# Query scores of the next batch ahead of this batch's key scores, in each pair of heads, in a cross-attention kernel

## The chip, the cores and the metric

The kernel runs on one core of one Trainium2 chip. The metric is the device time of one launch in microseconds (us); lower is better. The profile's span is the time from the first to the last recorded instruction of one execution.

## What is computed

For each of B = 16 batch entries: 256 query rows x of width 320, and 256 context rows of width 512, of which the first 248 are text keys and the last 8 are four "dummy" and four "ip" keys. There are 20 heads of 16.

```python
q = _split_heads(hidden_states @ w_q, HEADS)
k = _split_heads(text @ w_k, HEADS)
v = _split_heads(text @ w_v, HEADS)
out_text = _merge_heads(_sdpa(q, k, v))
mask_ip = _ip_mask(bbox, B, S, hidden_states.dtype)
k_ip = _split_heads(ip_h @ w_k_ip, HEADS)
v_ip = _split_heads(ip_h @ w_v_ip, HEADS)
out_ip = _merge_heads(_sdpa(q, k_ip, v_ip, mask=mask_ip))
out = out_text + IP_SCALE * out_ip
out = out @ w_out + b_out
out = out + residual
```

`_sdpa` is softmax(q k^T / 4 + mask) v, and each of the two softmaxes subtracts the maximum of its own keys.

## The kernel before, in words

Every value goes through TensorE in f32r, and precision is kept by splitting numbers into a high and a low part. The projections of batch entries to q, k and v are made for two entries at a time, in ten **tiles** per group (three of k, four of v, three of q; names `tile`, `k_tile`, `v_tile`, `q_tile`, lines 689 to 699). A tile of k or q is evacuated in two steps: ScalarE copies the high part (line 474), and VectorE, which waits for that copy, subtracts it from the accumulator to get the low part (line 587; lines 581 and 584 for a narrow tile). A v tile needs ScalarE alone (lines 467, 469). The parts go out to DRAM and come back as stacks (`q_stack`, `k_stack`, `stack2`) in which a pair of heads lies on 128 partitions, 64 for each.

Attention works on ten **pairs** of heads, p = 0 to 9, per batch entry t. Scores are made twice:

- **query scores** of entry t + 1 (`query_scores`, matmuls of line 743, queries on the partitions of the accumulator `score_q`): VectorE takes from them the maximum over each query's keys (`maxima`, lines 595 and 597). The maxima are turned and carried through DRAM into rows of the q stack, so that
- **key scores** of entry t (`key_scores`, matmuls of line 804, keys on the partitions, accumulator `score_t`) come out with the maximum and the mask already in them. ScalarE makes exp of them (line 520) into `probs`.

Each group of either kind is four matmuls of 256 columns with 64 rows of weights. `values` (line 819, 24 matmuls, once for two pairs, at even p) multiplies `probs` with v. ScalarE copies the result out (line 512), VectorE turns it and inverts the sums (lines 642, 645), GpSimd normalises (lines 434, 439), VectorE turns it back (line 650), TensorE projects (`project_out`, line 828), and VectorE adds the residual (line 657).

The order of all of it is written by hand in `batch(t)`, once for each engine, and every engine works its own list in order. On TensorE a pair p of step t is: key scores of (t, p); query scores of (t + 1, p); at even p the values; at p = 3, 5 and 9 the output projection of entry t - 1; at odd p, while t is up to 11 ("hosted"), a whole projection tile. On ScalarE a pair is: exp of the key scores, then (even p) the high part of a tile, then the copy of the values' result, then at some p the split of raw inputs (lines 454, 458). On VectorE it is: the maxima, at p = 4 and 9 a small turn (line 603), the low part of a tile, line 650, lines 642 and 645, line 657, and the split of inputs (lines 564, 568, 570) at p = 6 and 9 of odd t and p = 8 of even t.

The waits that tie them: a query group waits for `max_done`, the maxima of the pair before (for the pair before that one where there are two banks of `score_q`, entries 13 to 15, that is steps 12 to 14). A key group waits for `exp_done`, the exp of the pair before, since `score_t` is one buffer; at p = 0 and 5 also for the rows of maxima (`rows_loaded`). Values wait for the exp of pair p - 1. Query pair 1 of entry 13 also waits for the last two hosted tiles to be evacuated.

Of the kernel before, what the change touches and what calls it, by code (L numbers as in the profile page):

```python
# [34 lines left out]
def xattn(nc, x, xT, ctxT, ctx_sp, bbox, wq, wk, wv, wk_ip, wv_ip, wo, bias, grid, kaux, vones, out):  # L35
# [12 lines left out]
    with ctx:  # L48
# [67 lines left out]
        def double(b):  # L116
            return b == 0 or b - 1 > LAST_HOST
# [4 lines left out]
        def score_bank(b, p, e):  # L122
            return score_both(b, p)[:, 512 * e:512 * e + 512]
# [53 lines left out]
        def need(eng, s, value):  # L177
            if not isinstance(value, int) or value > 0:
                eng.wait_ge(s, value)
# [5 lines left out]
        def q_cols(w, p, e, a, n):  # L185
            return q_stacks[w][HEAD * e:HEAD * e + HEAD, p * S + a:p * S + a + n]
        def k_cols(w, p, e, a, n):
            return k_stacks[w][HEAD * e:HEAD * e + HEAD, p * KEYS + a:p * KEYS + a + n]
# [6 lines left out]
        def there(b):  # L195
            return 0 <= b < B
        def hosted(t):
            return -1 <= t <= LAST_HOST
# [5 lines left out]
        def tile_freed(eng, n):  # L204
            g, j = n // TILES, n % TILES
            if 3 <= j < 7:
                eng.wait_ge(v_evac, 4 * g + j - 2)
            else:
                eng.wait_ge(lo_done, 6 * g + (j if j < 3 else j - 4) + 1)
# [476 lines left out]
        def _(pe):  # L686
# [38 lines left out]
            def query_scores(b, p):  # L725
                n = PAIRS * b + p
                if p == 0:
                    pe.wait_ge(stack_loaded[b % 3], 112 * (b // 3 + 1))
                    if b == 0:
                        pe.wait_ge(kaux_loaded, 48)  # L730
                if p == 0 or not double(b):
                    need(pe, max_done, n)
                elif n - 1 > 0:
                    pe.wait_ge(max_done, n - 1)
                if p == 1 and b == 0:
                    for n_t in (12, 13):
                        tile_freed(pe, n_t)
                if p == 1 and b == LAST_HOST + 2:
                    for back in (1, 2):
                        tile_freed(pe, TILES * GROUPS - back)  # L740
                for tile in range(2):
                    for e in range(2):
                        last = mm(score_bank(b, p, e)[:, tile * KEYS:(tile + 1) * KEYS],  # L743
                                  q_cols(b % 3, p, e, tile * P, P), k_cols(b % 3, p, e, 0, KEYS), start=True, stop=True)
                last.then_inc(sq_ready, 1)
            def tile(n):
                g, j = n // TILES, n % TILES
                if g < 1 and j in (0, 3, 7):
                    pe.wait_ge(w_low, {0: 1, 3: 2, 7: 3}[j])
                if j == 7:  # L750
                    pe.wait_ge(x_tail, g + 1)
                if n < LONE:
                    if n >= 5:
                        tile_freed(pe, n - 5)
                else:
                    tile_freed(pe, n - (1 if n == LONE else 2))
                out = tile_bank(n)
                if j < 3:
                    k_tile(g, j, out)
                elif j < 7:  # L760
                    v_tile(g, j - 3, out)
                else:
                    q_tile(g, j - 7, out)
# [26 lines left out]
            def key_scores(b, p):  # L790
                if b == 0 and p == 0:
                    pe.wait_ge(max_done, PAIRS)
                if p % HALF == 0:
                    pe.wait_ge(rows_loaded[p // HALF], 16 * (b + 1))
                if b < B - 1 or p == 0:
                    need(pe, exp_done, PAIRS * b + p)
                elif p == 1:
                    pe.wait_ge(max_done, PAIRS * B)
                else:
                    pe.wait_ge(exp_done, PAIRS * b + p - 1)  # L800
                both = key_bank(b, p)
                for tile in range(2):
                    for e in range(2):
                        last = mm(both[:, 512 * e + S * tile:512 * e + S * tile + S],  # L804
                                  k_cols(b % 3, p, e, tile * P, P), q_cols(b % 3, p, e, 0, S), start=True, stop=True)
                last.then_inc(st_ready, 1)
            def values(b, k):
                u = b % 2
                if k == 0:
                    pe.wait_ge(v_spread, 2 * (b + 1))  # L810
                    pe.wait_ge(vsp_loaded[u], 8 * (b - u) + 16)
                need(pe, o_evac, QUADS * b + k)
                pe.wait_ge(exp_done, PAIRS * b + 2 * (k + 1))
                for kind in range(3):
                    tile = min(kind, 1)
                    for t in range(4):
                        a = (t % 2) * 2 * S + tile * S
                        at = S if kind == 2 else 0
                        last = mm(pv[32 * t:32 * t + 32, at:at + S], values_of(u, kind, 4 * k + t),  # L819
                                  probs[:, slot(u, 2 * k + t // 2), a:a + S],  # L820
                                  start=kind != 1, stop=kind != 0)
                last.then_inc(pv_ready, 1)
            def project_out(b, t, c):
                if t == 0:
                    pe.wait_ge(o_ready, OC * b + c + 1)
                if c == 0:
                    need(pe, out_done, OT * b + (t if b < B - 1 else 0))
                last = mm(out_bank(b, t), o_norm[:, b % 2, c, t * P:t * P + P], wo_sb[:, c, :],  # L828
                          start=c == 0, stop=c == OC - 1)
                if c == OC - 1:  # L830
                    last.then_inc(out_ready, 1)
            def batch(t):
                if t == 0:
                    pe.wait_ge(ld["small"], 32)
                    for back in range(1, 6):
                        tile_freed(pe, LONE - back)
                    pe.wait_ge(preset, 10)
                for p in range(PAIRS):
                    if there(t):
                        key_scores(t, p)  # L840
                    if there(t + 1):
                        query_scores(t + 1, p)
                    for k, off in VALUES.get(p, ()):
                        if there(t + off):
                            values(t + off, k)
                    for m, k in (OUT if t < B else LAST_OUT).get(p, ()):
                        if there(t - 1):
                            project_out(t - 1, m, k)
                    if hosted(t) and p % 2:
                        tile(5 * (t + 4) + p // 2)  # L850
            for t in range(-1, B + 1):
                batch(t)
# [57 lines left out]
```

## Time and profile before

| what | us |
|---|---|
| three runs | 506.11, 508.80, 510.87; median 508.8 |
| the profiled execution's own time | 508.77 |
| its span | 506.9 (1.9 us of the time lie outside it) |
| TensorE matmuls busy | 465.9 (92% of the span) |
| TensorE weight loads busy | 319.7 (63%) |
| VectorE busy | 391.2 (77%) |
| ScalarE busy | 275.3 (54%) |
| GpSimd busy | 154.1 (30%) |

PE is TensorE's matmuls, PEld its weight loads, DVE VectorE, ACT ScalarE, POOL GpSimd. Steps t = 0 to 15 begin with the key scores of their pair 0: step 1 at 108.66, step 3 at 166.16, step 4 at 193.09, step 12 at 419.45, step 13 at 440.35 and step 15 at 480.42.

### The profile page before, as it was taken

Reading aid. Unit: us, or ns where it says so; the run is one execution under the profiler, and the core shown is the slowest. Engines: PE = TensorE matmul, PEld = TensorE weight load, DVE = VectorE, ACT = ScalarE, POOL = GpSimd, SP = SyncE. Lnnn points to the kernel's source line nnn. Section 1 sums busy time; section 2 is a strip of 40 time slices with the busy share of each in tenths; the row PEclk is TensorE's granted clock in tenths of the full one; section 3 lists DMA queues with packets and bytes.
Section 4 is the critical chain, followed back from the end, with each engine's and each line's share of the span. In section 5 each row is a group of like instructions: output and inputs, shape, how many; then the busy total and the mean of one; then the engine's idle time right before and its main releaser. Section 6 shows DMA issues by size and latency. Waiting matters only on the chain.

```text
span 506.9 us, 11023 instructions
## 1 busy us (share of the span) xinstructions
PE 465.9 (92%) x4250; PEld 319.7 (63%) x4250; DVE 391.2 (77%) x705; ACT 275.3 (54%) x357; POOL 154.1 (30%) x242
## 2 busy tenths in 40 slices
PE   2899486999999999999999999999999998889987
PEld 2698364676666766676667766676667765555543
DVE  3824484796978789697978789697978788999933
ACT  3733022565646476456645566556645555666672
POOL 4490010313304152313204142323204141533442
PEclk9989695999999999999999999999999999999999
DMA  8989996929486585929495675939495655483021
GB/s 270 292 219 232 328 290 188 318 66 306 135 257 205 148 259 162 328 75 319 132 276 185 188 239 151 328 79 308 131 283 180 194 181 156 156 263 87 7 58 53
DMA packets 96453, 101.80 MB, mean 201 GB/s; under 512 B 16896, under 2 KB 83504, under 8 KB 96400
## 3 DMA queue, kind: packets, MB, share of 16 engines
q1 hardware_dynamic: 95408, 98.92, 63.1%
q0 software_dynamic: 992, 2.17, 2.0%
q8 instruction: 34, 0.56, 0.5%
q14 instruction: 19, 0.16, 0.1%
HBM read 67.87 MB, written 33.23 MB: 199 GB/s over the span
## 4 chain that ended last, share of the span: by engine, by line
PE 66%; DVE 14%; issue 7%; DMA 7%; ACT 3%; SPq 2%; POOL 1%; POOLq 0%; ACTq 0%
PE pv L819 15%; PE pj L828 10%; PE score_t L804 10%; PE score_q L743 6%; DVE max_cols L595 5%; PE score_q L694 4%; PE score_q L689 3%; PE score_q L695 3%; PE score_q L691 3%; PE score_q L696 3%; PE score_q L690 3%; PE score_q L698 2%; DVE qk_out L587 2%; PE score_q L699 2%; DMA v_rows<-v_out 1%
## 5 line engine op out<-in xcount | busy, mean ns | idle before, releaser
L520 ACT ACTIVATE probs<-score_t 128x1024 f32<-128x1024 f32 x155 | 158.3, 1021 | 139.5 <-PE score_t L804 139.2
L595 DVE TENSOR_REDUCE max_cols<-score_q 128x4 fp32r<-128x992 f32 x155 | 183.1, 1181 | 65.4 <-PE score_q L743 64.8
L819 PE MATMUL pv<-probs,v_cur 128*32 128x256 f32 x1920 | 120.2, 383 | 2.2 <-ACT probs L520 2.1
L434 POOL TENSOR_TENSOR o_turned<-o_turned,inv_cols 128x256 f32<-128x256 f32 x80 | 53.9, 674 | 158.0 <-DVE inv_cols L645 157.9
L819 PEld LDWEIGHTS pv<-probs,v_cur 128*32 128x32 f32 x1920 | 54.6, 109 | 40.6 <-issue 3.2
L426 POOL TENSOR_TENSOR x_all<-x_all,bias_sb 128x640 f32<-128x640 f32 x16 | 25.0, 1564 | 137.6 <-DMA x_all<-in_x 137.6
L828 PE MATMUL pj<-wo_sb,o_all 128*128 128x320 f32 x186 | 63.2, 460 | 4.0 <-DVE o_all L650 3.9
L512 ACT ACTIVATE o_all<-pv 128x512 f32<-128x512 f32 x80 | 47.8, 598 | 30.0 <-PE pv L819 29.3
L642 DVE STREAM_TRANSPOSE o_turned<-o_all 128x512 f32<-128x512 f32 x80 | 55.5, 693 | 10.9 <-ACT o_all L512 10.9
L804 PE MATMUL score_t<-q_stack,k_stack 64*128 64x256 f32 x420 | 52.9, 330 | 7.3 <-ACT probs L520 5.9
L804 PEld LDWEIGHTS score_t<-q_stack,k_stack 64*128 64x128 f32 x420 | 31.6, 186 | 44.3 <-issue 35.7
L743 PE MATMUL score_q<-k_stack,q_stack 64*128 64x256 f32 x420 | 44.4, 289 | 9.6 <-DMA q_stack<-aux_rows 7.5
L828 PEld LDWEIGHTS pj<-wo_sb,o_all 128*128 128x128 f32 x186 | 31.3, 189 | 19.5 <-DVE o_all L650 7.1
L743 PEld LDWEIGHTS score_q<-k_stack,q_stack 64*128 64x128 f32 x420 | 32.8, 188 | 12.7 <-issue 10.3
L689 PE MATMUL score_q<-wv_hl,c_hi 128*128 128x320 f32 x112 | 39.6, 353 | 0.0
L439 POOL TENSOR_TENSOR o_all<-o_turned 128x128 f32<-128x128 f32 x80 | 37.6, 469 | 6.3
L691 PE MATMUL score_q<-wv_hl,c_hi 128*128 128x320 f32 x112 | 35.3, 315 | 0.0
L690 PE MATMUL score_q<-wv_hl,c_lo 128*128 128x320 f32 x112 | 35.2, 314 | 0.0
L597 DVE TENSOR_REDUCE max_cols<-score_q 128x4 fp32r<-128x32 f32 x155 | 27.9, 180 | 0.0
L804 PEld LDWEIGHTS score_t<-stack 64*128 64x128 f32 x200 | 14.9, 184 | 20.1 <-issue 16.6
L804 PE MATMUL score_t<-stack 64*128 64x256 f32 x200 | 25.2, 330 | 2.1 <-ACT probs L520 2.1
L474 ACT ACTIVATE qk_out<-score_q 128x512 fp32r<-128x512 f32 (+1 forms) x40 | 23.5, 588 | 3.8 <-PE score_q L695 3.3
(163 smaller groups left out, 683.3 us busy)
## 6 DMA issues: line engine op xcount, KB each, us to landing
k_stack<-k_parts SPq DMA_DIRECT2D x33, 320.0 KB, 5.0
q_stack<-q_parts SPq DMA_DIRECT2D x33, 320.0 KB, 5.5
q_parts<-qk_out SPq DMA_DIRECT2D x32, 256.0 KB, 4.7
k_parts<-qk_out SPq DMA_DIRECT2D x32, 248.0 KB, 5.2
raw<-in_ctxT SPq DMA_DIRECT2D x14, 512.0 KB, 4.5
v_rows<-v_out SPq DMA_DIRECT2D x32, 160.0 KB, 5.0
v_stage<-v_rows SPq DMA_DIRECT2D x16, 320.0 KB, 6.2
x_all<-in_x SPq DMA_DIRECT2D x16, 320.0 KB, 6.1
```

The costliest lines, as they stand in the source:

```text
L434: pool.tensor_tensor(out, out, inv_cols[:, n % SLOTS, :].unsqueeze(2).broadcast_to([P, 2 * S // 32, DH]), ALU.mult).then_inc(scaled, 1)
L512: nc.scalar.activation(o_raw[:, n % SLOTS, :], pv[:, :], ACT.Copy).then_inc(o_evac, 1)
L520: nc.scalar.activation(probs[:, slot(t % 2, p), :], key_bank(t, p), ACT.Exp, scale=SCALE)\
L595: nc.vector.tensor_reduce(out=max_cols[:, h, :, at:at + 4:2].rearrange("p t e -> p e t"), in_=both[:, :, :, 0:TEXT], op=ALU.max, axis=AX.X ...
L642: nc.vector.transpose(turned_blocks(n), o_raw[:, n % SLOTS, :].rearrange("p (j n) -> p j n", n=32))\
L689: mm(out, w_hi, x_hi_, start=start, stop=False)
L690: mm(out, w_lo, x_hi_, start=False, stop=False)
L691: return mm(out, w_hi, x_lo_, start=False, stop=stop)
L743: last = mm(score_bank(b, p, e)[:, tile * KEYS:(tile + 1) * KEYS], q_cols(b % 3, p, e, tile * P, P), k_cols(b % 3, p, e, 0, KEYS), start=T ...
L804: last = mm(both[:, 512 * e + S * tile:512 * e + S * tile + S], k_cols(b % 3, p, e, tile * P, P), q_cols(b % 3, p, e, 0, S), start=True, s ...
L819: last = mm(pv[32 * t:32 * t + 32, at:at + S], values_of(u, kind, 4 * k + t), probs[:, slot(u, 2 * k + t // 2), a:a + S], start=kind != 1, ...
L828: last = mm(out_bank(b, t), o_norm[:, b % 2, c, t * P:t * P + P], wo_sb[:, c, :], start=c == 0, stop=c == OC - 1)
```

## The change

In the pair loop of TensorE's `batch` the query scores of entry t + 1 stand ahead of the key scores of entry t. Nothing else is touched: the same instructions, waits and buffers, and the lists of the other engines are as before.

```diff
@@ -836,10 +836,10 @@
                         tile_freed(pe, LONE - back)
                     pe.wait_ge(preset, 10)
                 for p in range(PAIRS):
+                    if there(t + 1):
+                        query_scores(t + 1, p)
                     if there(t):
                         key_scores(t, p)
-                    if there(t + 1):
-                        query_scores(t + 1, p)
                     for k, off in VALUES.get(p, ()):
                         if there(t + off):
                             values(t + off, k)
```

## Rows read from the trace of the kernel before

**Rows 1.** The profile's page, part 1: TensorE's share of the span.
```profile
PE 465.9 (92%) x4250; PEld 319.7 (63%) x4250; DVE 391.2 (77%) x705; ACT 275.3 (54%) x357; POOL 154.1 (30%) x242
```
**Rows 2.** Windows of steps 3, 4 and 13: length, busy by engine, clock, DMA.
```profile
166.16:193.09 26.93, 26.85 (x259) 18.28 (x258) 22.34 (x43) 16.82 (x22) 8.72 (x14) 1.00 0.71 224
193.09:222.81 29.72, 29.23 (x271) 20.17 (x270) 25.11 (x45) 16.31 (x21) 8.41 (x13) 1.00 0.65 199
...
440.35:460.38 20.03, 17.94 (x213) 10.77 (x213) 18.75 (x39) 12.68 (x15) 7.61 (x13) 1.00 0.54 170
```
**Rows 3.** Waits from 109 to 419 us: total, times, longest.
```profile
PE pj L828 <- DVE o_all L650: 2.4, 5, 0.5
PEld score_q L743 <- DVE max_cols L597: 1.7, 6, 0.3
```
**Rows 4.** Timeline of TensorE, pairs 6 to 9 of step 3: start, length.
```profile
182.06 0.51 PE L804 MATMUL score_t<-q_stack,k_stack 64*128 64x256 f32 x4
182.41 0.40 PE L743 MATMUL score_q<-k_stack,q_stack 64*128 64x256 f32 x4
182.73 1.50 PE L819 MATMUL pv<-probs,v_cur 128*32 128x256 f32 x24
...
186.88 0.51 PE L804 MATMUL score_t<-q_stack,k_stack 64*128 64x256 f32 x4
187.24 0.51 PE L743 MATMUL score_q<-k_stack,q_stack 64*128 64x256 f32 x4
187.67 1.50 PE L819 MATMUL pv<-probs,v_cur 128*32 128x256 f32 x24
...
189.69 0.50 PE L743 MATMUL score_q<-k_stack,q_stack 64*128 64x256 f32 x4
190.12 0.81 PE L828 MATMUL pj<-wo_sb,o_all 128*128 128x320 f32 x2
```
**Rows 5.** Timeline of ScalarE, pair 6 of step 3.
```profile
182.61 1.03 ACT L520 ACTIVATE probs<-score_t 128x1024 f32<-128x1024 f32 x1 [1.22 <-PE score_t L804]
183.53 0.59 ACT L474 ACTIVATE qk_out<-score_q 128x512 fp32r<-128x512 f32 x1
```
**Rows 6.** Timeline of VectorE, pairs 6 to 8 of step 3.
```profile
182.85 1.19 DVE L595 TENSOR_REDUCE max_cols<-score_q 128x4 fp32r<-128x992 f32 x1 [1.00 <-PE score_q L743]
183.96 0.18 DVE L597 TENSOR_REDUCE max_cols<-score_q 128x4 fp32r<-128x32 f32 x1
184.16 0.69 DVE L587 TENSOR_TENSOR qk_out<-score_q,qk_out 128x512 fp32r<-128x512 f32 x1
184.77 1.22 DVE L564 TENSOR_TENSOR c_lo<-raw,c_hi 128x1024 fp32r<-128x1024 f32 x1
...
187.00 0.18 DVE L597 TENSOR_REDUCE max_cols<-score_q 128x4 fp32r<-128x32 f32 x1
...
189.45 0.18 DVE L597 TENSOR_REDUCE max_cols<-score_q 128x4 fp32r<-128x32 f32 x1
```
**Rows 7.** Timeline of TensorE, pair 9 of step 4.
```profile
218.80 0.50 PE L743 MATMUL score_q<-stack 64*128 64x256 f32 x4
```
**Rows 8.** Timeline of TensorE: query groups that waited, entries 1 and 2.
```profile
82.51 0.80 PE L743 MATMUL score_q<-k_stack,q_stack 64*128 64x256 f32 x4 [0.75 <-DVE max_cols L597]
...
109.66 0.50 PE L743 MATMUL score_q<-stack 64*128 64x256 f32 x4 [0.49 <-DVE max_cols L597]
```
**Rows 9.** Timeline of TensorE, step 12: query pair 1, projection at pair 3.
```profile
423.13 0.50 PE L743 MATMUL score_q<-k_stack,q_stack 64*128 64x256 f32 x4 [1.08 <-issue]
...
427.41 0.81 PE L828 MATMUL pj<-wo_sb,o_all 128*128 128x320 f32 x2 [0.47 <-DVE o_all L650]
```
**Rows 10.** Timeline of step 13: key groups of pairs 1 and 2, and exp between.
```profile
442.45 0.50 PE L804 MATMUL score_t<-q_stack,k_stack 64*128 64x256 f32 x4
...
443.08 1.02 ACT L520 ACTIVATE probs<-score_t 128x1024 f32<-128x1024 f32 x1
...
444.15 0.50 PE L804 MATMUL score_t<-q_stack,k_stack 64*128 64x256 f32 x4 [0.96 <-ACT probs L520]
```

## Prediction, made before the changed kernel was run

> **What bounds the kernel now.** First the busy shares of the page: TensorE's matmuls fill 92% of the span, VectorE 77%, ScalarE 54% [rows 1]. Since that is an average over stages, the second view is the windows by step. In steps 3 and 4, which have projection tiles in them, TensorE is busy 26.85 of 26.93 us and 29.23 of 29.72, VectorE 83% and 84%; in step 13, which has none, 17.94 and 18.75 of 20.03 [rows 2]. So steps 1 to 11 belong to TensorE: anything that makes it stand still is paid in full there. The last full steps are a chain among three engines. The third view is the waits of 109 to 419 us: query groups wait for maxima six times, 1.7 us in all, and the projection five times for line 650, 2.4 us [rows 3]. VectorE's wait for query scores is not on the path. The fourth view, the timelines, shows how close these waits are, and carries the sum.
>
> **What the swap moves.** No instruction is added. A key group starts at 182.06, the query group at 182.41, the values at 182.73: whichever group is first takes 0.34, the second 0.33, 0.67 together [rows 4]. Both have four matmuls of 256 columns with 64 rows of weights, so I take the same steps with the names exchanged. Then query scores end 0.23 earlier in a pair and key scores 0.23 later: the first group ends 0.51 after the pair's start, the second 0.75 (182.41 + 0.40 - 182.06 = 0.75; 0.75 - 0.51 = 0.24, and 0.23 between the starts of what reads them) [rows 4]. In TensorE's sum that is nothing. The question is who reads late or early.
>
> **Part 1, the wait that moves ahead of the key scores (steps 1 to 10).** Look at pairs 6 to 8 of step 3. ScalarE makes exp of pair 6 from 182.61, and only behind it the high part of the tile, 183.53 to 184.12 [rows 5]. VectorE ends its maxima of pair 6 at 184.14, starts the low part at 184.16, then the input split at 184.77, and so ends the maxima of pair 7 at 187.18; the query group of pair 8 starts at 187.24, 0.06 later [rows 4, 6]. Two things had to be ready for the low part at 184.16, the maxima (184.14) and the high part (184.12). The swap makes the first 0.23 earlier, as VectorE waited 1.00 us for the query scores [rows 6], and the second 0.23 later, because exp starts later. The later one decides: low part, split and maxima of pair 7 are all 0.23 late, and the maxima end at 187.41. Before, the key group (186.88) ran while TensorE waited for these maxima, and the values followed the query group by 0.43 (187.24 to 187.67) [rows 4]. Now the key group stands behind the wait: query 187.47, key 187.81, values 187.47 + 0.67 = 188.14. That is 0.47 late: 0.23 from the late exp, 0.24 from the lost cover.
>
> At pair 9 VectorE comes without a gap from the same chain, the maxima of pair 8 ending at 189.45 + 0.18 = 189.63. The query group moves from 189.69 to 189.92, and what follows from 190.12 to 190.59, again 0.47 in absolute time, so it is not paid twice [rows 4, 6]. From there to the next such place TensorE has its tile to do, VectorE catches up, and at pair 6 of the next step it again waits for the query scores. So the loss comes once in a step. In an even step the narrow tile stands in the place of tile and split, and it is at pair 9 that the query group waits (0.50 long, as a stalled one is, against 0.40) [rows 7]: 0.47 there too. In step 11 there is no input split, so I count nothing. Ten steps x 0.47 = **4.7 us**. The bounds: nothing, if the low part isn't late (then the 0.23 gained by the maxima just pays for the lost cover); 10 x 0.67 = 6.7, if a whole pair of groups is lost. I take 4.7, since both inputs of the low part are within 0.04 us of its start in the row.
>
> The projection of pair 5 waits for line 650, behind a low part [rows 3]. Between nothing and 5 x 0.23 = 1.2 us; the maxima ahead of it come 0.23 sooner, which nearly makes room for the later high part, so I take **0.3**.
>
> **Part 2, steps 0 and 1.** Query pair 1 of entry 1 waits for its maxima and starts at 82.51 [rows 8]; the key group of that step ran ahead of it, in idle time, and now follows. That costs between 0.34 and, the group there being 0.80 long where a stalled one elsewhere has 0.50 [rows 4, 8], about twice that; part comes back later, so **0.35**. At 109.66 pair 0 of entry 2 waits in the same way for maxima behind a split [rows 8]: 0.23 + 0.24 = **0.47**. Together 0.8 (bounds 0.3 and 1.2).
>
> **Part 3, steps 12 to 14.** In step 13 the key group of pair 2 (444.15) waits 0.96 for the exp of pair 1, which starts at 443.08, 0.13 after the end of the key group of 442.45 (442.95), where exp elsewhere follows by 0.04 (182.57 to 182.61): ScalarE is held by its copy of the values' result [rows 4, 5, 10]. After the swap that key group ends at 443.18 and exp starts at 443.23, 0.15 late. The next query group is then made inside the wait, so the values follow a lone key group by 0.43 instead of 0.67. Gain 0.67 - 0.43 - 0.15 = 0.09, at three of the five pairs of pairs: 0.27 in each of two steps, **-0.5**. If VectorE alone bounded these steps, 20.03 could fall towards its 18.75 [rows 2]: at most 1.3 each.
> Step 12 loses. Query pair 1 of entry 13 waits for the last tile's evacuation until 423.13 [rows 9], and the key group and its exp used to lie in that wait. Now they follow it: key, exp (1.02) and a lone key group before the values add up to about 1.5. The projection of pair 3 stood 0.47 for line 650 [rows 9] and more waits for exp follow, and VectorE is nearly full there, so most is absorbed: between 0 and 1.5, I take **+0.5**. The tail comes out at 0 (bounds -2.6 and +1.5). Step 15 has no query scores.
>
> **Sum.** 4.7 + 0.3 + 0.8 + 0 = +5.8 us on the profiled execution's 508.77 (its span and 1.9 us around it): **514.6 us**, +1.1%. That execution lies on the median of the runs shown, 508.8.
>
> **A page's rule against the rows.** VectorE at 83% is in step 3 well below TensorE's matmuls, but above its weight loads, 18.28 of 26.93 us or 68% [rows 2]. The Trainium skill, "Perfetto Trace Analysis", section "Identifying the Most-Contended Engine", says that busy matmuls are a bad measure of TensorE's headroom and that weight-load occupancy should be used. By it VectorE would be the contended engine and TensorE would have room for the late starts, and the sum would be near zero; by the rows, groups that follow one another without a gap, there is none. That is rival B.
>
> **The rivals.**
> A. The low part isn't late, since TensorE's ends in the trace are modelled and 0.04 us decides. Then maxima of pair 7 end at 186.95, query pair 8 starts at 187.01, and values at 187.68, as before; the same at pair 9. Parts 2 and 3 remain: about 509.6. For it: nothing but the smallness of the margin. Against: ScalarE works in order, and exp starts 0.04 after the key scores' end.
> B. The hosted steps have slack and nothing moves: 508.8. For it the share of weight loads; against it 26.85 of 26.93 us.
> C. Faster. In the last steps and wherever VectorE waits for query scores it gains 0.23 a pair. The mechanism is one: the maxima are VectorE's longest work, and if their chain set the pace of steps 12 to 14, these would fall from 20.0 towards 18.75 us, 3 x 1.3 = 3.9 us less, 505. It decides only if exp (ScalarE) isn't what holds pair 2 and if the hosted steps lose nothing; the row shows the wait for exp.
> D. The new standstills of steps 0, 1 and 12 bring TensorE's clock down from 2.4 to 1.2 GHz for a stretch. In the rows shown for the full steps the granted clock is 1.00, with hardly an idle microsecond [rows 2]; step 12 would have one idle stretch of about 1.6 us ahead of its second query group (1.08 in the row, and the 0.50 of the key group that leaves it) [rows 4, 9]. The price if some 4 to 7 us of matmuls run at half speed: 3 us more, 517.6.
>
> **How the numbers follow.** Forecast 0.68, A 0.14, B 0.05, C 0.05, D 0.08. A measurement of this kernel tells about 1%, 5.1 us, from no change, so the border is 513.9, close under the forecast. Of the forecast I put seven tenths above it (the hosted loss could as well be 4 as 5.5): 0.49, with D 0.57. Faster by over 1% needs all of C and more: 0.02. The rest, 0.41, is within 1%. The range: below it B and C, above it half of D; 509.3 to 517.2.
>
> **What would show it.** In the changed profile: (1) query group first in each pair, 0.34 to the key group; (2) at pair 6 of odd steps the tile's high part 0.23 later after the pair's start (1.47 to 1.70), the low part right behind it, with a small idle gap ahead of it on VectorE; (3) at pairs 8 and 9 idle time of TensorE ahead of the query group for maxima, and a total of such waits from 109 to 419 us of some 5 us more than 1.7; (4) step 3 at 27.4 and step 4 at 30.2 us; (5) step 13 at about 19.8; (6) values of step 12's first pairs 1.5 us late, mostly made good by its end. It would be wrong if steps 3 and 4 keep 26.9 and 29.7 (A or B), if low parts still start with the maxima's end (A), if steps 13 and 14 lose more than a microsecond each (C), or if a stretch at half clock appears past 109 us (D).

## The result, and the profile after

| | kernel before | changed kernel |
|---|---|---|
| median of 4 runs each, us | 508.07 | 514.92 |
| lowest and highest | 506.11, 510.87 | 513.68, 516.63 |
| span of the profiled execution | 506.9 | 512.5 |

The ratio of the times is 1.0133, with a 95% interval of 1.0074 to 1.0192: slower by 1.3%. The forecast was 514.6 us.

The busy shares of the page have hardly moved: the same work, spread over 5.6 us more.

```profile
span 512.5 us, 11023 instructions
...
PE 465.7 (91%) x4250; PEld 319.8 (62%) x4250; DVE 391.5 (76%) x705; ACT 281.0 (55%) x357; POOL 153.1 (30%) x242
```

The windows of steps 3, 4, 12 and 13 of the changed kernel (length, then the busy time of PE, PEld, DVE, ACT, POOL, the granted clock, DMA share and GB/s):

```profile
167.18:194.82 27.64, 26.57 (x258) 18.14 (x257) 22.61 (x43) 17.11 (x22) 7.97 (x14) 1.00 0.68 218
194.82:225.23 30.41, 29.42 (x269) 20.04 (x269) 25.23 (x45) 16.66 (x21) 8.23 (x13) 1.00 0.65 195
424.96:446.47 21.51, 18.10 (x213) 10.85 (x212) 19.47 (x38) 13.66 (x16) 7.62 (x13) 1.00 0.56 172
446.47:466.28 19.81, 18.04 (x213) 10.82 (x213) 18.69 (x38) 13.22 (x15) 7.61 (x13) 1.00 0.53 172
```

Steps 3 and 4 were 26.93 and 29.72 us with TensorE busy nearly throughout; they are now 27.64 and 30.41, and TensorE stands still for about a microsecond in each (1.07 and 0.99, against 0.08 and 0.49 before [rows 2]). Step 13 is 0.22 shorter than its 20.03 [rows 2]; step 14 went from 20.04 to 19.79. Step 12 went from 20.90 to 21.51. Step 11 has kept its 26.44.

What TensorE now waits for, from 109 to 425 us (total, times, longest):

```profile
PEld score_q L743 <- DVE max_cols L597: 34.5, 68, 1.2
...
PE score_q L743 <- DVE max_cols L597: 7.2, 20, 0.8
DVE qk_out L587 <- ACT qk_out L474: 6.9, 17, 0.5
PEld pj L828 <- DVE o_all L650: 5.7, 10, 0.8
DVE tail_rest L581 <- ACT qk_out L474: 4.4, 10, 0.5
...
PE pj L828 <- DVE o_all L650: 2.9, 5, 0.6
```

The matmuls of query groups wait for maxima twenty times, in every one of steps 1 to 10 and mostly twice, for 7.2 us in all. The row to set beside it, from 109 to 419 us of the kernel before, is that of the matmuls too:

```profile
PE score_q L743 <- DVE max_cols L597: 0.5, 1, 0.5
```

VectorE waits for the high part of a tile, 11.3 us over 27 times, which did not stand among the waits of before at all. (The weight loads' own total of 34.5 counts idle time of weight loads while matmuls still run, and isn't lost time. The 1.7 us in six waits of [rows 3] is such a row of weight loads.)

The timelines of pairs 6 to 9 of step 3 show the chain. TensorE:

```profile
183.07 0.50 PE L743 MATMUL score_q<-k_stack,q_stack 64*128 64x256 f32 x4
183.41 0.40 PE L804 MATMUL score_t<-q_stack,k_stack 64*128 64x256 f32 x4
183.75 1.50 PE L819 MATMUL pv<-probs,v_cur 128*32 128x256 f32 x24
...
188.74 0.50 PE L743 MATMUL score_q<-k_stack,q_stack 64*128 64x256 f32 x4 [0.79 <-DVE max_cols L597]
189.08 0.40 PE L804 MATMUL score_t<-q_stack,k_stack 64*128 64x256 f32 x4
189.41 1.50 PE L819 MATMUL pv<-probs,v_cur 128*32 128x256 f32 x24
...
191.19 0.50 PE L743 MATMUL score_q<-k_stack,q_stack 64*128 64x256 f32 x4 [0.28 <-DVE max_cols L597]
```

ScalarE, then VectorE:

```profile
183.85 1.02 ACT L520 ACTIVATE probs<-score_t 128x1024 f32<-128x1024 f32 x1 [1.28 <-PE score_t L804]
184.77 0.59 ACT L474 ACTIVATE qk_out<-score_q 128x512 fp32r<-128x512 f32 x1
```

```profile
184.72 0.18 DVE L597 TENSOR_REDUCE max_cols<-score_q 128x4 fp32r<-128x32 f32 x1
185.40 0.69 DVE L587 TENSOR_TENSOR qk_out<-score_q,qk_out 128x512 fp32r<-128x512 f32 x1 [0.49 <-ACT qk_out L474]
186.00 1.48 DVE L564 TENSOR_TENSOR c_lo<-raw,c_hi 128x1024 fp32r<-128x1024 f32 x1
187.41 1.18 DVE L595 TENSOR_REDUCE max_cols<-score_q 128x4 fp32r<-128x992 f32 x1
188.51 0.18 DVE L597 TENSOR_REDUCE max_cols<-score_q 128x4 fp32r<-128x32 f32 x1
```

Pair 6 starts at 183.07. Exp starts 0.78 after it (0.55 before [rows 4, 5]), the high part 1.70 after it (1.47 before), and the low part 2.33 after it, where it was 2.10 [rows 4, 6]. VectorE is free at 184.90 and stands 0.49 until the high part is there; before, the two came 0.02 apart. The query group of pair 8 starts 0.05 after the end of the maxima, with nothing ahead of it but idle time, and the key group is behind it.

### The profile page after: what moved, and what is told of

It reads as the page before. It is cut to its first block, busy times and chain, and to the rows that moved or that the text cites. A ratio compares the mean times of both kernels' runs of the same rounds, so it can differ in the third digit from the quotient of the medians.

```text
span 512.5 us, 11023 instructions
## 1 busy us (share of the span) xinstructions
PE 465.7 (91%) x4250; PEld 319.8 (62%) x4250; DVE 391.5 (76%) x705; ACT 281.0 (55%) x357; POOL 153.1 (30%) x242
## 4 chain that ended last, share of the span: by engine, by line
PE 64%; DVE 15%; issue 8%; DMA 6%; ACT 4%; SPq 1%; POOL 1%; POOLq 0%; ACTq 0%; DVEq 0%
PE pv L819 13%; PE pj L828 10%; PE score_q L743 10%; DVE max_cols L595 6%; PE score_t L804 6%; PE score_q L694 4%; PE score_q L695 3%; PE score_q L689 3%; PE score_q L696 3%; PE score_q L691 3%; PE score_q L690 3%; ACT qk_out L474 2%; PE score_q L698 2%; PE score_q L699 2%; DMA max_rows<-row_buf 2%
## 5 line engine op out<-in xcount | busy, mean ns | idle before, releaser
L743 PE MATMUL score_q<-k_stack,q_stack 64*128 64x256 f32 x420 | 53.4, 333 | 17.1 <-DVE max_cols L597 10.1
L512 ACT ACTIVATE o_all<-pv 128x512 f32<-128x512 f32 x80 | 47.8, 598 | 12.8 <-PE pv L819 11.3
L804 PE MATMUL score_t<-q_stack,k_stack 64*128 64x256 f32 x420 | 43.1, 283 | 3.5 <-ACT probs L520 3.5
L743 PEld LDWEIGHTS score_q<-stack 64*128 64x128 f32 x200 | 14.9, 185 | 21.5 <-DVE max_cols L597 14.4
L743 PE MATMUL score_q<-stack 64*128 64x256 f32 x200 | 25.0, 328 | 3.3 <-DVE max_cols L597 3.1
```

The costliest lines, as they stand in the source:

```text
L512: nc.scalar.activation(o_raw[:, n % SLOTS, :], pv[:, :], ACT.Copy).then_inc(o_evac, 1)
```

## The experiments

Step lengths below are read from key and query group starts in each trace. In the even steps up to 10 and in steps 11 and 14 they repeat between traces of the same order to a few hundredths, where whole times spread over 4 us, so most verdicts rest on them. Odd steps need one more number beside them, given below the table. All kernels use this scheme in the pair loop, with another condition in each:

```diff
+                    first = <condition>
+                    if there(t + 1) and first: query_scores(t + 1, p)
                     if there(t): key_scores(t, p)
+                    if there(t + 1) and not first: query_scores(t + 1, p)
```

| kernel, condition for query scores first | step 3 | step 4 | step 12 | step 13 | step 14 |
|---|---|---|---|---|---|
| before: never | 26.93 | 29.72 | 20.90 | 20.03 | 20.04 |
| changed: always | 27.65 | 30.41 | 21.52 | 19.81 | 19.79 |
| e1: not at pairs 8, 9 | 27.52 | 30.19 | 23.32 | 20.04 | 20.03 |
| e2: always; high part ahead of exp | 27.05 | 29.50 | 21.14 | 20.05 | 19.79 |
| e3: never; high part ahead of exp | 26.80 | 29.71 | 20.90 | 20.03 | 20.04 |
| e4: steps 13, 14 | 27.06 | 29.72 | 20.91 | 19.81 | 19.79 |
| e5: pair 6 of steps 1 to 10 | 27.15 | 29.91 | 20.90 | 20.04 | 20.03 |
| e6: pairs 8, 9 of steps 1 to 10 | 27.14 | 29.98 | 20.90 | 20.03 | 20.04 |
| e7: see below | 26.77 | 29.54 | 20.91 | 19.81 | 19.79 |
| e8: not in step 12 | 27.38 | 30.38 | 20.90 | 19.81 | 19.79 |
| e9: step 0 and pair 0 of step 1 | 27.19 | 29.72 | 20.90 | 20.05 | 20.03 |
| e10: steps 1 to 10 | 27.40 | 30.40 | 21.74 | 20.04 | 20.03 |
| e11: step 12 | 26.91 | 29.71 | 23.08 | 20.04 | 20.03 |

Odd steps vary by more than even ones, also where nothing was changed. They go with the length of the input split behind pair 6 (line 564): with the order of before in it, step 3 is 26.91 to 26.93 where that split took 1.22, 27.06 where it took 1.36 (e4), and 27.19 where it took 1.48 (e9). So odd steps are compared here at equal splits. The split of step 3 took 1.22 in the kernel before, e5, e6, e8, e10 and e11, 1.21 in e3, and 1.48 in the changed kernel, 1.59 in e1, 1.46 in e2 and 1.43 in e7.

**Giving back one half: key scores first at pairs 8 and 9.**

```diff
+                    first = p not in (8, 9)
```

> The change with the key scores first again at pairs 8 and 9 alone. Theory: the 0.47 us that a hosted step loses are two halves. One is that exp of the key scores, and behind it on ScalarE the tile's high part at pair 6, start 0.23 late; the other is that at pairs 8 and 9 the key group no longer covers the wait for the maxima. This kernel gives back the second half only. So step 3 (27.65 in the changed kernel, 26.93 before) comes to 27.2 to 27.4, step 4 (30.41, 29.72 before) to about 30.15, and at pair 6 the high part is still 1.7 us after the pair's start. Rival (the lost cover is all of it, the late exp harmless): steps 3 and 4 are back at 26.9 and 29.7.

The windows of steps 3 and 4:

```profile
168.47:195.99 27.52, 26.98 (x260) 18.27 (x259) 22.72 (x43) 17.21 (x22) 8.62 (x14) 1.00 0.68 219
195.99:226.17 30.18, 29.52 (x269) 20.08 (x269) 25.16 (x45) 16.56 (x21) 8.42 (x13) 1.00 0.65 196
```

Steps 5 and 7 are at 27.15, against 27.38 in the changed kernel and 26.91 and 27.16 before (step 7 of before has a split of 1.47); even steps at 30.16 to 30.22. Step 3 lies above the range expected, with a split that took 1.59 where steps 5 and 7 have 1.22. So the cover gives back 0.2, and a loss stays: the rival, that the cover is all of it, falls. The single time was 516.59 us, above the changed kernel's, because of steps 0 and 12; step 12 is taken up under e11.

**The two halves each by itself.** First pair 6 alone, then pairs 8 and 9 alone.

```diff
+                    first = 1 <= t <= 10 and p == 6
```

> Query scores first at pair 6 of steps 1 to 10 alone, the kernel before elsewhere. Nothing stands behind a wait that did not before, so only the late exp is left, which is 0.23 us at pair 6. Theory: the tile's high part and the low part behind it are 0.23 late, so are the maxima that pairs 8 (odd steps) and 9 (even steps) wait for: step 3 comes to 27.16 (or 0.25 more if its input split is one of the long ones) and step 4 to 29.95, 0.23 above the kernel before in each. Rival (the lost cover is all that costs): 26.93 and 29.72.

VectorE at pairs 6 and 7 of step 3:

```profile
183.23 0.18 DVE L597 TENSOR_REDUCE max_cols<-score_q 128x4 fp32r<-128x32 f32 x1
183.91 0.69 DVE L587 TENSOR_TENSOR qk_out<-score_q,qk_out 128x512 fp32r<-128x512 f32 x1 [0.49 <-ACT qk_out L474]
184.51 1.22 DVE L564 TENSOR_TENSOR c_lo<-raw,c_hi 128x1024 fp32r<-128x1024 f32 x1
```

The same 0.49 of waiting as in the changed kernel, at a single exchanged pair in the step. Step 3 is +0.22, step 4 +0.19. The single time was 509.89.

```diff
+                    first = 1 <= t <= 10 and p in (8, 9)
```

> Query scores first at pairs 8 and 9 of steps 1 to 10 alone. Theory: the chain through pair 6 is on time, and the key group no longer covers the wait for maxima: 0.24 a step, step 3 at about 27.17, step 4 at about 29.96. With the kernel that swaps pair 6 alone it adds up to the 0.47 forecast for a step. Rival (the late exp is all of it): 26.93 and 29.72.

Step 3 is +0.21, step 4 +0.26; the single time was 511.89. In step 3, with the same split of 1.22 in all three, the halves add up to 0.43, close to what a step was forecast to lose (0.47). In step 4 they add up to 0.45, while the full swap costs 0.69. The other 0.2 is not made at pairs 6, 8 or 9; it is taken up in the part on the prediction.

**Taking the late exp out of the low part's way.** On ScalarE, in the changed kernel, the tile's evacuation goes ahead of exp:

```diff
                 for p in range(PAIRS):
+                    n = tile_due(t, p) if t >= 0 or p else LONE - 1
+                    if n is not None:
+                        tile(n)
                     if there(t):
...
-                    n = tile_due(t, p) if t >= 0 or p else LONE - 1
-                    if n is not None:
-                        tile(n)
```

> The change, and on ScalarE at even pairs the tile's high part ahead of exp. Theory: the high part is then done before the maxima end, the low part starts with the maxima's end, 0.23 us earlier than before the change, and this gain pays for the lost cover. Steps 3 and 4 come to about 26.9 and 29.6 (27.65 and 30.41 in the changed kernel), and the time falls by 4.5 to 6 us against it, to 509 to 510.5: not above the kernel before by more than 0.5%. Exp at even pairs starts 0.1 us later or less, which nobody waits for. Rival (the lost cover is the whole loss): step lengths and time stay as in the changed kernel, 514 to 515.

Ten runs gave a median of 506.6 us against 508.55 for the kernel before, ratio 0.9975 (0.9952 to 0.9998), a result better than expected, though the interval reaches nearly to 1. ScalarE and VectorE at pair 6 of step 3 (in e2, e3 and e7 exp is L523):

```profile
181.16 0.60 ACT L474 ACTIVATE qk_out<-score_q 128x512 fp32r<-128x512 f32 x1 [0.60 <-PE score_q L695]
181.83 1.02 ACT L523 ACTIVATE probs<-score_t 128x1024 f32<-128x1024 f32 x1
```

```profile
182.70 0.18 DVE L597 TENSOR_REDUCE max_cols<-score_q 128x4 fp32r<-128x32 f32 x1
182.80 0.68 DVE L587 TENSOR_TENSOR qk_out<-score_q,qk_out 128x512 fp32r<-128x512 f32 x1
183.40 1.46 DVE L564 TENSOR_TENSOR c_lo<-raw,c_hi 128x1024 fp32r<-128x1024 f32 x1
```

The low part follows the maxima at once: it starts 1.75 after the pair's start, against 2.33 in the changed kernel and 2.10 before. Even steps fall to 29.48 to 29.50, below the 29.7 of before; odd steps lie between 26.79 and 27.08, those with a split of 1.22 or 1.23 at 26.79 and 26.80. So the loss is gone once nothing else holds the low part. Step 12 is 21.14. Step 13 has kept 20.05: its first key group starts 0.48 after the query group instead of 0.34, since its rows of maxima had not yet landed.

**The control: the same exchange in the kernel before.**

> Control: the kernel before, with the same exchange on ScalarE. Theory: there the low part of pair 6 is held by the maxima's end just as much (184.14 against 184.12 for the high part), so nothing is gained: steps 3 and 4 at 26.9 and 29.7, time within 0.4% of the kernel before. Rival (the high part held VectorE in the kernel before too, and the exchange gains by itself): 2 to 5 us less than before, in steps 1 to 10.

Ratio 1.0000 (0.9978 to 1.0022), and even steps as before, 29.70 to 29.74: the exchange on ScalarE gains nothing that whole times can tell. It isn't quite without effect. In step 3 the low part starts 1.99 after the pair's start instead of 2.10, so in the kernel before the high part held it by 0.1, and odd steps with a split of 1.21 are 26.79 and 26.80 against 26.90 to 26.93, some 0.12 less. Five such steps make 0.6 us, inside the interval.

Beside e3 the result of e2 reads more closely. In odd steps both have 26.80: there the swap gains nothing, its earlier maxima just paying for the lost cover. In even steps the swap brings 29.71 down to 29.50, and 0.21 of this is there by the start of pair 6 (18.28 after the step's start, against 18.49). It is the wait of the projection of pair 5. From 109 to 417 us, e3 first and e2 second:

```profile
PE pj L828 <- DVE o_all L650: 2.5, 5, 0.5
PE pj L828 <- DVE o_all L650: 1.3, 5, 0.3
```

**The last steps alone.**

```diff
+                    first = t in (13, 14)
```

> Query scores first in steps 13 and 14 alone. Theory: steps 0 to 12 have the lengths of the kernel before (within 0.1 us), steps 13 and 14 fall from 20.03 to 19.8, since exp starts 0.15 us late but the query group is made while TensorE waits for it; the time is 0.4 to 0.5 us below before, which no pair of runs can tell, only the step lengths. Rival (the gain in the last steps needs what the earlier steps changed): steps 13 and 14 at 20.0.

Steps 13 and 14 are 19.81 and 19.79, all others as before (507.67 us in one run). The gain of 0.22 and 0.25 belongs to these steps and needs nothing from the others. TensorE in step 13 of the changed kernel shows how it comes about:

```profile
448.92 0.40 PE L804 MATMUL score_t<-q_stack,k_stack 64*128 64x256 f32 x4
449.15 0.40 PE L743 MATMUL score_q<-stack 64*128 64x256 f32 x4
450.44 0.50 PE L804 MATMUL score_t<-q_stack,k_stack 64*128 64x256 f32 x4 [0.88 <-ACT probs L520]
450.87 1.50 PE L819 MATMUL pv<-probs,v_cur 128*32 128x256 f32 x24
```

The query group of pair 2 (449.15) is made in what was a wait for exp, and the values follow the key group by 0.43. Before, that wait was idle [rows 10].

**Step 12.** First the change without it:

```diff
+                    first = t != 12
```

> The change without step 12. Theory: step 12 is 20.9 again (21.5 in the changed kernel), because the key group and its exp lie again in the wait of the second query group; steps 13 and 14 keep 19.8; steps 1 to 10 keep the changed kernel's lengths. About 0.6 us less than the changed kernel. Rival (step 12's loss comes from what the steps before left late, not from the order in it): 21.5 stays.

Step 12 is 20.90, as before the change, so its loss comes from the order in it. (The single time, 516.02, carries a step 0 of 34.4 us.) Then step 12 alone:

```diff
+                    first = t == 12
```

> Query scores first in step 12 alone. Theory: step 12 at 21.5 instead of 20.9, +0.6 us in time, which 5 rounds tell at best just. Rival (the idle stretch ahead of the second query group brings the clock down in some executions, as in the kernel with the key scores first at pairs 8 and 9, where step 12 took 23.3 with a half-clock stretch in it): a mean price above 1 us, and single executions that are 1.8 us longer.

Twelve runs: median 509.51 against 508.55, ratio 1.0018 (0.9996 to 1.0041). The execution that was profiled shows the rival's case. Windows of its step 12, the eighth column being the granted clock:

```profile
419.50:423.20 3.70, 1.17 (x18) 0.94 (x14) 3.22 (x6) 1.75 (x3) 0.00 (x0) 0.98 0.24 56
...
423.10:426.50 3.40, 3.40 (x28) 1.45 (x28) 2.30 (x5) 1.02 (x1) 1.08 (x2) 0.50 0.84 249
426.50:440.47 13.97, 13.09 (x144) 7.86 (x140) 12.76 (x26) 9.57 (x11) 5.50 (x9) 1.00 0.57 188
```

and its TensorE:

```profile
421.21 0.50 PE L743 MATMUL score_q<-k_stack,q_stack 64*128 64x256 f32 x4 [1.65 <-issue]
...
423.06 0.80 PE L804 MATMUL score_t<-q_stack,k_stack 64*128 64x256 f32 x4 [0.88 <-ACT probs L520]
423.79 2.79 PE L819 MATMUL pv<-probs,v_cur 128*32 128x256 f32 x24
```

TensorE stood idle for 1.65 us and again for 0.88, was busy 1.17 of 3.70 us, and then its clock was 0.50, that is 1.2 GHz, for 3.4 us: the values took 2.79 us instead of 1.50. Step 12 came to 23.08, of which 0.62 is the order (21.52 - 20.90) and some 1.6 the clock. e1 shows the same, 23.32 with a clock of 0.52 from 430.6 to 434.0. In the profiled execution of the changed kernel itself TensorE did the same before this point, and the clock stayed at 1.00:

```profile
427.07:430.77 3.70, 1.17 (x18) 0.93 (x16) 3.22 (x6) 1.75 (x3) 0.00 (x0) 1.00 0.24 57
```

In e2, with idle stretches of 1.27 and 0.88 there, it stayed up as well. So the fall comes in some executions and not in others. How often isn't shown: the twelve times of e11 lie between 508.41 and 513.52 and don't fall into two groups.

**Step 0 alone.**

```diff
+                    first = t == 0 or (t == 1 and p == 0)
```

> Query scores first in step 0 and at pair 0 of step 1 alone. Theory of the prediction: +0.8 us (509.2 against 508.4), since the key groups of these two places no longer run inside a wait. Rival: from the start of step 0 to pair 2 of step 1 the kernels with the old order there took 36.7 to 38.1 us, and three with the new order 37.8, 39.2 and 39.6, so the price is nearer to 1.6 us; or this is the spread of the loads and of the clock's half-speed stretch there, and the price is nothing that 5 rounds can tell (under 0.2%).

Median 508.86 against 508.55, ratio 1.0011 (0.9990 to 1.0031). That is +0.5 us with an interval from -0.5 to +1.6: it agrees with 0.8 and can't be told from nothing; a price of 1.6 is at its edge. From the start of step 0 to pair 2 of step 1 the kernels with the old order there took 36.7 to 38.1 us, those with the new order 36.9 to 39.6 (e9 itself 37.5), and e10, which has the new order in step 1 but not in step 0, 38.3. What makes that spread wasn't tried.

**Steps 1 to 10 alone.**

> Query scores first in steps 1 to 10 alone. Theory: the whole hosted loss and nothing else, steps 2 to 10 as in the changed kernel (27.4 and 30.4), +4.9 us in step lengths, time 513 to 513.8 against 508.4, ratio 1.009 to 1.011; steps 12 to 14 as before the change. Rival (steps 0 and 12 to 14 carry a good part of the 5 to 7 us measured): ratio under 1.008.

```diff
+                    first = 1 <= t <= 10
```

Ratio 1.0101 (1.0060 to 1.0142), median 513.80 against 508.55: +5.2 us, nearly all of what the change costs, and its step lengths are those of the changed kernel. Its step 12, untouched by the edit, was 21.74. The pairs of this step lie where they did in the kernel before, and the time is lost at its end, where the first key group of step 13 waits for its rows of maxima to come back from DRAM:

```profile
448.96 0.50 PE L804 MATMUL score_t<-q_stack,k_stack 64*128 64x256 f32 x4 [0.77 <-DMA q_stack<-max_rows]
```

The transfer that loads them was issued 19.64 us after the start of step 12, where the kernel before issued it after 18.21. Why it was late in this execution isn't shown.

**A version of it all.** High part ahead of exp; query scores first where it pays:

```diff
+                    first = t != 12 and not (t % 2 and t < 12 and p in (8, 9))
```

> High part ahead of exp on ScalarE; query scores first, but not in step 12 and not at pairs 8 and 9 of the odd steps up to 11. Theory: even steps keep the 29.48 that the kernel with the high part first has; odd steps gain the 0.23 as well, since maxima are earlier and the key group covers the wait again: about 26.7; step 12 is back at 20.9, steps 13 and 14 at 19.8. Together some 3 us less than the kernel before, 505 to 506.3, ratio 0.993 to 0.996. Rival (the 0.23 is lost elsewhere on VectorE): odd steps stay at 26.9 and the time at that of the kernel with the high part first, 506.6.

Twelve runs, median 505.71 us against 508.37, ratio 0.9952 (0.9935 to 0.9968). The windows of steps 4, 5 and 12:

```profile
193.92:223.46 29.54, 29.22 (x269) 20.12 (x268) 25.21 (x45) 17.23 (x21) 8.44 (x13) 1.00 0.66 201
223.46:250.02 26.56, 26.56 (x259) 18.23 (x259) 21.99 (x43) 17.73 (x22) 7.77 (x14) 1.00 0.71 227
418.50:439.41 20.91, 18.16 (x214) 10.72 (x214) 19.13 (x38) 13.16 (x16) 7.32 (x13) 1.00 0.58 177
```

Step 5 has no idle time of TensorE left. With its split of 1.22 it is 0.23 under the odd steps of e2 and e3, since the key group covers the wait for the maxima again: the earlier maxima are now a gain there too. Even steps are 29.53 to 29.57, slightly above the 29.48 expected. The kernel has the lowest median of those run, 0.5% under the kernel before.

## Why the prediction was right, and where it was off

*Part 1, steps 1 to 10.* Right in mechanism and nearly in size. The low part was late as computed (2.33 after the pair's start instead of 2.10), the query group of pair 8 waited, and the key group stood behind it. The odd steps with an input split of 1.22 us, as in the row of before, came to 27.38 against 26.91 to 26.93, +0.45 to +0.47. e5 and e6 show the halves, 0.22 and 0.21 in step 3. e2 and e3 show that rival A's arithmetic was right too, for a kernel in which the low part isn't late: then odd steps neither lose nor gain by the swap. One reading was off: for the waits of query groups the prediction took the row of weight loads, 1.7 us in six waits, where the matmuls waited once, for 0.5; its sign of some 5 us more is to be set against that (7.2 now). In even steps pair 8 waited too, for 0.15 to 0.18, and not pair 9 alone.

Rival B had for it that weight loads fill only 68% of a hosted step. The late starts were paid in full all the same. By the rule of the Trainium skill, "Perfetto Trace Analysis", section "Identifying the Most-Contended Engine", which judges TensorE's headroom by weight loads and by the share of peak work (MFU, not worked out here), such starts had room; here they had none. What the same section of the Trainium skill says against the busy share of matmuls as a measure is borne out in part: step 5 was 26.82 busy of 26.91 us before, and in e7 the same work was 26.56 busy of 26.56. So about 0.3 us of the busy time before was not work that had to be done, and a share of 99.7% did not mean that nothing could be won.

*The projection of pair 5, the term that was mis-sized.* I took 0.3 us in all, between bounds of 0 and 1.2; it came out near the upper one. Even steps lost 0.62 to 0.70 instead of 0.53, that is some 0.2 beyond the 0.47 in each, or 1.0 in five. In step 4 pair 4 starts 0.12 later after the step's start than before, and pair 6 0.23 later. TensorE and VectorE of the changed kernel at pairs 3 and 5:

```profile
203.34 1.46 PE L828 MATMUL pj<-wo_sb,o_all 128*128 128x320 f32 x4
...
210.95 0.81 PE L828 MATMUL pj<-wo_sb,o_all 128*128 128x320 f32 x2 [0.58 <-DVE o_all L650]
```

```profile
202.90 0.69 DVE L587 TENSOR_TENSOR qk_out<-score_q,qk_out 128x512 fp32r<-128x512 f32 x1 [0.49 <-ACT qk_out L474]
203.50 0.43 DVE L650 STREAM_TRANSPOSE o_all<-o_all 128x256 f32<-128x256 f32 x1
```

The four matmuls of pair 3 take 1.46 us where they took 1.34, since line 650 stands behind a low part that waits 0.49 for its high part, at pair 2 as at pair 6. I had looked for such a place at pair 5 only, and had let the earlier maxima make up for it; they can't, for the low part waits for ScalarE and not for them. The failure is a smaller form of the same mechanism in a place that I had not followed. That this chain decides the wait is shown from the other side: with the high part ahead of exp the wait for line 650 falls from 0.49 to 0.25 under the swap (e2), and stays 0.49 without it (e3). How the extra 0.2 is shared among pairs 2, 4 and 5 is only read from the traces; no kernel moved pairs 2 and 4 alone.

*Part 2, steps 0 and 1.* Forecast 0.8. In the traces it is +0.9 (37.80 - 36.92), from the start of step 0 to pair 2 of step 1, but e9 gives 0.5 with an interval that holds 0. Open beyond that.

*Part 3, steps 12 to 14.* -0.22 and -0.25 in steps 13 and 14 against -0.27 each; +0.62 in step 12 against +0.5. Right, the second by a share that was judged between far bounds. The values of pair 2 in step 12 were 1.52 late (6.11 after the step's start instead of 4.59), as forecast, and most of it was made good by the step's end.

*Rival D.* Its mechanism exists, at the place named, in some executions. It was given 3 us, and costs 1.6 where it was seen. It reckoned with one idle stretch of 1.6 (1.65 in the trace); the wait of 0.88 behind it was not foreseen.

*The sum in the traces.* Part 1 from pair 2 of step 1 to the start of step 11 is +5.6 (5.0 forecast), part 2 +0.9 (0.8), step 12 +0.6 (0.5), steps 13 and 14 -0.5 (-0.5). That is +6.6. Step 0 happened to start 0.96 earlier in the trace of after (76.37 against 77.33, in a range of 75.3 to 78.8 over all kernels), so the spans differ by 5.6. The measured ratio stands for +6.8, with an interval from 3.8 to 9.8 us. That the forecast time lies only 0.3 from the measured median is in part luck: it added 5.8 to an execution of 508.77, and the four runs of the kernel before have a median of 508.07.

## What to carry to other kernels

When two independent groups of equal length on the bound engine are exchanged, that engine's sum doesn't change: look up, for each group, the first reader and what stands behind that reader on its in-order engine. Here what counted was not exp, which nobody waited for, but the copy queued behind it. And a group that needs nothing late is worth most right where its engine waits: putting the group with the wait first gives that cover away, unless the wait becomes shorter by as much. Once the copy was taken from behind exp, the same swap turned from a loss of 1.3% into a small gain (0.25%, with an interval from nearly 0 to 0.5%).

## What was not expected of the hardware

The input split of line 564 (128 x 1024 values on VectorE) behind pair 6 takes 1.21 or 1.22 us in about half of the odd steps and up to 1.59 in the others, with no change in its code; step 3 of the changed kernel was one of the long ones (1.48), and it is the difference between its 27.65 and the 27.38 of its neighbours. In the 65 such splits of the thirteen traces, the 31 with no GpSimd instruction beside them all took 1.21 or 1.22, and all 30 that took 1.23 or more had one of lines 421, 434 or 439 beside them; but four that had one took 1.21 or 1.22 too. So an overlap goes with every long split and isn't enough by itself. What makes it long is open; no kernel moved the GpSimd instructions.

The granted clock fell to 0.50 for 3.4 us in step 12 of two kernels' profiled executions after TensorE had been busy 1.17 of 3.70 us with no single idle stretch above 1.65, and did not fall in a third, the changed kernel, after the same 1.17 of 3.70.
